# Attention slots rebuilt around three batches at a time, weights and rows transposed by DMA

## What is computed

```python
x = x + tanh(g_xattn[0]) * xattn(layernorm(x), ctx_512, Wq, Wkv_expand, Wout)
x = x + tanh(g_ffn[0]) * ffn(layernorm(x), w_gate_up, w_down)

# xattn: 16 heads of 32, causal, softmax over the keys
qp, (k, v) = q @ Wq.T, split(latent_kv @ Wkv_expand.T)
attn = softmax(where(causal, (qh @ kh.T) / sqrt(32), lowest)); out = (attn @ vh) @ Wout.T
# ffn, I = 1408; every operand is rounded to 255 steps of its row's maximum
gate, up = split(quant(x) @ quant(w_gate_up).T)
return quant(silu(gate) * up) @ quant(w_down).T
```

## Time and profile before

| what | us |
|---|---|
| time, median of 3 runs (lowest, highest) | 884.68 (880.06, 885.18) |
| the profiled execution's own time | 884.49 |
| its span, from the first to the last instruction | 882.4 |
| busy: PE 782.7 (89%), DVE 638.7 (72%), POOL 518.5 (59%), ACT 418.2 (47%) | of 882.4 |
| mean granted TensorE clock | 0.955 of full |

### The profile page before, as it was taken

One profiled execution on the slowest core, in us unless ns is written; L12 is line 12 of the kernel. 1 busy time (PEld: TensorE's weight loads), 2 busy tenths in 40 slices (PEclk: granted clock), 3 DMA queues, 4 the chain that ended last, 5 costly groups with the idle time before them and its releaser, 6 DMA issues. The chain is left out here.

```text
span 882.4 us, 19003 instructions
## 1 busy us (share of the span) xinstructions
PE 782.7 (89%) x6146; PEld 564.8 (64%) x6168; DVE 638.7 (72%) x1997; ACT 418.2 (47%) x664; POOL 518.5 (59%) x671
## 2 busy tenths in 40 slices
PE   2579899998999989989999999897699999999994
PEld 2468787886877877868878778675444444444441
DVE  3575776876866867768678576476389999999992
ACT  5336456466375464563664645414234444444441
POOL 3525466474564663754745637324167888888885
PEclk9788899999999999999999999977899999999998
DMA  5784765775857757768668575406115655565666
GB/s 211 176 195 130 173 164 150 179 191 140 212 150 180 173 161 164 179 147 204 168 164 190 144 179 124 125 2 269 61 23 117 160 151 140 139 139 139 144 140 168
DMA packets 121889, 135.98 MB, mean 154 GB/s; under 512 B 73536, under 2 KB 84288, under 8 KB 121536
## 3 DMA queue, kind: packets, MB, share of 16 engines
q1 hardware_dynamic: 120768, 134.26, 60.0%
q10 hardware_dynamic: 1024, 0.53, 0.2%
HBM read 47.06 MB, written 25.30 MB: 82 GB/s over the span
## 5 line engine op out<-in xcount | busy, mean ns | idle before, releaser
L654 DVE CUSTOM_DVE_ANT_0 junk<-psum,mask 128x128 f32<-128x128 f32 (+1 forms) x512 | 159.4, 354 | 5.0 <-PE psum L843 3.2
L1172 PE MATMUL psum<-w1q,xqb 128*128 128x512 bf16 (+1 forms) x757 | 157.7, 363 | 3.3 <-PEq L255 1.9
L1072 POOL TENSOR_TENSOR up<-gate,up 128x512 f32<-128x512 f32 (+1 forms) x96 | 112.4, 1185 | 46.1 <-ACT gate L1098 38.3
L390 POOL TENSOR_SCALAR_AFFINE_SELECT prob<-prob 128x512 f32<-128x512 f32 x128 | 80.2, 638 | 94.5 <-ACT prob L588 87.0
L1172 PEld LDWEIGHTS psum<-w1q,xqb 128*128 128x128 bf16 x768 | 75.4, 98 | 83.9 <-issue 4.0
L1103 ACT ACTIVATE up<-up,round_bias,hinv 128x1408 f32<-128x1408 f32 x32 | 50.0, 1561 | 128.7 <-DVE hinv L1144 128.7
L588 ACT ACTIVATE prob<-psum 128x768 f32<-128x768 f32 x128 | 101.5, 827 | 18.4 <-PE psum L912 18.0
L910 PE MATMUL psum<-qs,ks 98*128 98x256 f32 x256 | 78.8, 369 | 23.8 <-DMA qs<-nmT 18.6
L1186 PE MATMUL psum<-w2q,hqT 128*128 128x512 bf16 x341 | 81.8, 389 | 7.4 <-DMA hqT<-hq 6.8
L910 PEld LDWEIGHTS psum<-qs,ks 98*128 98x128 f32 x256 | 50.8, 199 | 44.6 <-DMA qs<-nmT 25.9
L843 PE MATMUL psum<-ks,qs 96*128 96x256 f32 x256 | 76.1, 344 | 0.0
(11 more groups left out here) (126 smaller groups left out, 1904.2 us busy)
## 6 DMA issues: line engine op xcount, KB each, us to landing
ks<-k_hi SPq DMA_DIRECT2D x128, 128.0 KB, 2.7
qs<-q_hi SPq DMA_DIRECT2D x128, 128.0 KB, 2.4
xln<-x_dram SPq DMA_DIRECT2D x16, 512.0 KB, 5.0
ks<-k_lo SPq DMA_DIRECT2D x64, 128.0 KB, 2.5
qs<-q_lo SPq DMA_DIRECT2D x64, 128.0 KB, 2.9
x<-x_dram SPq DMA_DIRECT2D x16, 512.0 KB, 3.9
x_scratch<-x SPq DMA_DIRECT2D x16, 512.0 KB, 5.1
x1b<-x_scratch SPq DMA_DIRECT2D x32, 256.0 KB, 3.5
```

Of the source, the lines that this page charges most:

```text
L390: pool.affine_select(out=blk, in_=blk, compare_op=ALU.is_ge, fill=0.0, base=0, pattern=[[0, 4], [1, P]], channel_multiplier=-1).then_inc(s ...
L654: dve.tensor_tensor_reduce(junk[:, n % 2, 0:w], psum[:, h % 4, cols], m, 1.0, LOWEST, ALU.add, ALU.max, mx[:, par, t, h:h + 1]).then_inc(s ...
L1072: pool.tensor_tensor(up[:, t % 3, o], gate[:, t % 3, o], up[:, t % 3, o], ALU.mult).then_inc(f["prod_done"], 1)
L1172: last = pe.matmul(psum[:, n, 0:w], xqb[:, t % 4, k, :], w1q[:, k, half * I + o:half * I + o + w], start=(k == 0), stop=(k == KH - 1))
```

## The change

Slots run from b = -2 to 16, all with whole numbers. In slot b there are now batch A = b in the pairs, N = b + 1 in the scores and maxima, F = b + 2 in normalisation, transposes and all projections, T = b - 1 in the output projection. Scores use banks 0 and 1 (head h waits for the maxima of head h - 2), pairs banks 2 and 3 (each pair waits for the exponential before). Both phases stand interleaved on TensorE; the scores begin behind the fourth pair. The bf16 transposes of xq and of weight pieces on TensorE, their copies on VectorE, and the 26 scale matmuls go away: pieces are stored as they are, and `dma_start_transpose` loads w1q, w2q and each `xqb`; the scales go through DRAM and come back as broadcast rows. The weights lie where the projections' operands lay, so they are loaded in slot 14, when the last q, k and v are made. Both blocks become one, and tile 0 of the feed-forward stands between slots 15 and 16. `stand_alone` (a semaphore increment behind some waits) goes.

```diff
-            for b in range(-3, B + 2):
-                slot(b, b % 2, b // 2)
+        def run(eng, slot, tile):
+            for b in range(-2, B):
+                slot(b)
+            tile(0)
+            slot(B)
+            for t in range(1, NT + 4):
+                tile(t)
...
-        WORK = [("K", 0, 1), ("K", 1, 1), ("Q", 0, 1), ("BC", 0, -1), ("BC", 1, -1), ("Q", 1, 1), ("V", 0, 1),
-                ("XT", 0, -2), ("O", 0, -1), ("O", 1, -1), ("V", 1, 1), ("XT", 1, -2), ("T", 0, 2), ("T", 1, 2),
-                ("W", 0, 1), ("W", 1, 1)]
+        WORK = [("O", 0, -1), ("O", 1, -1), ("T", 0, 2), ("T", 1, 2), ("K", 0, 2), ("K", 1, 2), ("Q", 0, 2),
+                ("BC", 0, 0), ("Q", 1, 2), ("BC", 1, 0), ("V", 0, 2), ("V", 1, 2)]
```

```diff
+                def load_x(tile):
+                    sp.wait_ge(s["xq_stored"], DMA * (tile // ST + 1))
+                    sp.dma_start_transpose(xqb[:, tile % 4], xq_scratch[tile]).then_inc(f[f"x_loaded{tile % 4}"], DMA)
...
+                    if b == B - 2:
+                        sp.wait_ge(s["q_moved"], DMA * MOVES * B)
+                        sp.wait_ge(s["k_moved"], DMA * MOVES * B)
+                        sp.wait_ge(s["v_done"], 2 * B)
...
+                        sp.dma_start_transpose(w1q[:], w1_scratch).then_inc(f["w1_loaded"], DMA)
+                        sp.dma_start(s1[:], rows[:, 0:2 * I].broadcast_to((P, 2 * I))).then_inc(f["steps_loaded"], DMA)
+                        sp.dma_start(s2[:], rows[:, 2 * I:NW * P].broadcast_to((P, H))).then_inc(f["steps_loaded"], DMA)
+                        sp.dma_start_transpose(w2q[:], w2_scratch).then_inc(f["w2_loaded"], DMA)
+                        for tile in range(2):
+                            load_x(tile)
```

The order of a slot on GpSimd:

```diff
+                    split_context()
+                    rsqrt1()
+                    weights()
+                    if b == -2:
+                        tables()
+                    select(0)
+                    select(1)
+                    low_t(0)
+                    select(2)
+                    select(3)
+                    low_t(1)
+                    select(4)
+                    rsqrt2()
+                    select(5)
+                    low_k(0)
+                    select(6)
+                    select(7)
+                    low_k(1)
+                    low_o(0)
+                    quantise(0)
+                    low_o(1)
+                    quantise(1)
```

On ScalarE:

```diff
+                    if b > -2:
+                        weights()
+                    exps(0)
+                    norm1(0)
+                    exps(1)
+                    norm1(1)
+                    exps(2)
+                    high_t(0)
+                    exps(3)
+                    copy_u(0)
+                    exps(4)
+                    high_t(1)
+                    exps(5)
+                    norm2(0)
+                    copy_u(1)
...
+                    exps(6)
+                    high_k(0)
+                    exps(7)
+                    norm2(1)
+                    copy_u(2)
+                    high_k(1)
+                    copy_u(3)
+                    high_q(0)
+                    maxima_rows()
+                    high_o(0)
+                    high_q(1)
+                    high_o(1)
+                    copy_v(0)
+                    copy_v(1)
```

On VectorE:

```diff
+                    measure_x()
...
+                    residual(0)
+                    measure(0)
+                    residual(1)
+                    measure(1)
+                    for h in range(12):
+                        maxima(h)
+                    reciprocals()
+                    maxima(12)
+                    maxima(13)
+                    split_q(0)
+                    maxima(14)
+                    maxima(15)
+                    negate()
+                    step(0)
+                    normalise(0)
+                    split_q(1)
+                    normalise(1)
+                    step(1)
+                    weigh_rows(b + 3)
```

On TensorE, the wait of `scores(h)`, that of `score_pair(pair)`, and the order:

```diff
+                            wait_for(pe, s["max_done"], 2 * (NHEAD * N + h - 1))
...
+                        wait_for(pe, s["exp_done"], PAIRS * A + pair)
...
+                    output(0, 0)
+                    output(0, 1)
+                    score_pair(0)
+                    output(1, 0)
+                    score_pair(1)
+                    output(1, 1)
+                    score_pair(2)
+                    transposed(0)
+                    score_pair(3)
+                    weigh(0)
+                    scores(0)
+                    scores(1)
+                    score_pair(4)
+                    transposed(1)
+                    scores(2)
+                    scores(3)
+                    score_pair(5)
+                    weigh(1)
+                    scores(4)
+                    scores(5)
+                    score_pair(6)
+                    keys(0)
+                    scores(6)
+                    scores(7)
+                    score_pair(7)
+                    weigh(2)
+                    scores(8)
+                    scores(9)
+                    keys(1)
+                    scores(10)
+                    scores(11)
+                    weigh(3)
+                    queries(0)
+                    scores(12)
+                    scores(13)
+                    queries(1)
+                    scores(14)
+                    scores(15)
+                    queries(2)
+                    maxima_rows()
+                    broadcast(0)
+                    queries(3)
+                    broadcast(1)
+                    values(0)
+                    values(1)
```

More of the change, by code:

```diff
@@ new lines, in gated_block @@
+        mx = keep("mx", [P, 2, ST, NHEAD], F32)
+        nm = keep("nm", [P, ST, 2, NHEAD], F32R)
+        nmT = keep("nmT", [2 * NHEAD, S], F32R)
+        prob = keep("prob", [P, 2, 2, CAUSAL // P, 2, P], F32)
+        u = keep("u", [P, GROUPS, S], F32)
+        o_hi = keep("o_hi", [P, GROUPS, S], F32R)
+        o_lo = keep("o_lo", [P, GROUPS, S], F32R)
+        rec = keep("rec", [P, S], F32)
+        rec_hi = keep("rec_hi", [P, S], F32R)
+        rec2 = keep("rec2", [P, S], F32R)
+        x1 = keep("x1", [P, ST, H], F32)
@@ L337, in _ @@
+                run(sp, slot, tile)
+                for p in range(2):
+                    sp.wait_ge(f[f"stored{p}"], DMA * NT // 2)
             @block.gpsimd
@@ L422, in slot @@
-                    first = isinstance(b, int) and b == -2
-                    if first:
-                        split_context()
-                    if present(b + 1):
-                        for m in range(2):
-                            pool.wait_ge(s["k_copied"], 2 * (b + 1) + m + 1)
-                            wait_for(pool, s["k_moved"], DMA * MOVES * (b + 1))
-                            pool.tensor_tensor(k_lo[:, 2 * m:2 * m + 2, :], both[:, 2 * m:2 * m + 2, :],
-                                               k_hi[:, 2 * m:2 * m + 2, :].bitcast(F32), ALU.subtract).then_inc(s["k_lo"], 1)
@@ L1094, in silu, with tile @@
+                def tile(t):
                     def silu(c):
@@ L1106, in slot, with low_weights @@
                     silu(2)
-                run_tiles(act, slot)
+                run(act, slot, tile)
             @block.vector
             def _(dve):
-                dve.wait_ge(f["steps"], NSTEPS)
-                def slot(t):
+                dve.memset(round_bias[:], ROUND).then_inc(s["table"], 1)
+                def low_weights(n, hi, lo, raw):
+                    dve.wait_ge(s["high"], n + 1)
+                    dve.tensor_tensor(lo[:], raw, hi[:].bitcast(F32), ALU.subtract).then_inc(s["split"], 1)
@@ L1188, in slot @@
                         last.then_inc(f["d_done"], 1)
-                run_tiles(pe, slot)
+                run(pe, slot, tile)
 def kernel(x, ctx_512, g_xattn, g_ffn, L0_xattn_Wq, L0_xattn_Wkv_expand, L0_xattn_Wout, L0_ffn_w_gate_up,
```

1272 lines of the change are left out of this document (538 added, 734 removed).

## The result

The changed kernel takes 945.27 us (median of 4 runs, 944.4 to 946.37) where the kernel before takes 884.93 (4 runs, 880.06 to 886.74): ratio 1.0695, 95% interval 1.0657 to 1.0734. It is about 7% slower. The forecast was 897.0 with a range up to 932, so the sign was right and the size far off. The profiled execution has a span of 943.5 us.

What follows compares the result with a forecast made beforehand. Attention slots paced by TensorE's matmul starts plus handoff waits, 36.7 us each: 64.4 + 513.8 + 59.4 = 637.6 to the first feed-forward matmul, plus 246.7 + 10.6 gives span 894.9, plus 2.1 gives 897.0 us; range 858 to 932.

Steps and rivals of the forecast that it cites:

- The slot by handoffs: One attention slot followed engine by engine: 28.9 us of TensorE work plus 7.7 of stalls, the two ways meeting at 36.5.
- First stretch: Slot's start, work banks 6 and 7: TensorE waits for split_q(1) ahead of values(0); stall 2.1 us in all.
- Second: Score pairs 0 to 5, each waiting for the exponential before it, and weigh(0): stall 1.6 us.
- Third stretch: GpSimd's late rsqrt2 delays norm2(0) on ScalarE, hence exps(6) and pair 7 on TensorE: stall 2.5 us.
- rival A: GpSimd reaches rsqrt2 3.1 us earlier, the third stall goes: slot 34.4 us, 865 us in all; chance 0.24.
- Rival B: Waits merely change places, the slot stays 35.2 us as before: 876 us in all; chance 0.14.
- Fourth: Slot's end: split_q(0) holds queries(2), the end of the maxima holds their transposition: stall 1.5 us.
- I put one in ten here: TensorE's half clock behind pair 7's still stretch, assumed in one slot of ten: 0.2 us a slot.
- Rival C: TensorE's clock falls in every slot, +2.0 us each: 925 us in all; chance 0.14.
- 59.4 together: Slots 14 and 15, which lack projections, taken as 32 and 27.4 us up to tile(0).
- the paragraph on SyncE: SyncE's queue in a slot: 24 head spreads, 15 us, the last queries' hidden by 2.6 us; xq's store behind them.
- rival D: Transposed weights come late for the feed-forward: 7 us, 904 us in all; chance 0.08.

Runs made afterwards that it cites:

- e3: The changed kernel with GpSimd doing rsqrt2 ahead of low_t(1) and select(4) instead of behind them: 908.59 us.
- e7: On e5, the slot's last stretch reordered: queries(2) in the other work bank, values(0) ahead of broadcast(1), q_hi(1) and v(0) copied earlier: 900.70 us.
- e10: On e9, last stretch reordered: broadcast(0) ahead of scores(14), normalise(0) ahead of maxima(14), split_q(0) behind the negation, both low_o ahead of quantise: 872.80 us.
- e11: On e10, in slot -2 GpSimd rounds weights behind low_t(1) and writes the tables behind low_k(1): 867.39 us.
- e9: On e4, the scales are turned by TensorE and stored as 26 rows of 512 bytes instead of 3,328 elements of 4 bytes: 878.58 us.
- e1: The changed kernel with VectorE gating w2's scales in slot 4, not at the end of slot 13; store unmoved: 924.08 us.
- e2: The changed kernel with the scale store moved to the end of SyncE's slot 13, its wait kept: 931.78 us.
- e12: On e9, three extra unread stores of constants: 512 elements in slot 4, 3,328 in slot 7, 128 rows of 104 bytes in slot 10: 883.78 us.
- e4: The changed kernel with both edits of e1 and e3 (w2's scales gated in slot 4, rsqrt2 early): 886.40 us.
- e5: On e4, the scale store cut up: two columns in each w1 piece's slot, w2's four in slot 5: 898.23 us.
- e6: On e5, in slot -2 GpSimd rounds weights behind low_t(1) and writes the tables behind low_k(1): 894.07 us.

## Why the prediction was right or wrong

The slot by handoffs: right. Without a fall of the clock it takes 36.79 us, forecast 36.5. First stretch: the gap ahead of values(0) is 1.77 us, forecast 1.76 (0.24 to 2.0). Second: pair 3 starts 12.3 us behind the last queries, forecast 12.5. Third stretch: GpSimd's rsqrt2 holds norm2(0) by 2.88 us and pair 7 by 1.95, forecast 3 and 2.5, and e3 shows it as a cause: with rsqrt2 ahead of low_t(1) the slot is 34.55. That is rival A's number, 34.4; its condition, GpSimd 3.1 us earlier, wasn't met. Rival B fell with the same rows. Fourth: 1.02 us at queries(2), in the changed kernel as in e3, forecast 1.5 for the whole stretch. e7 and e10 show that these waits aren't worth their length: with them moved or shortened, the slot was no shorter.

The clock: mechanism right, size wrong. "I put one in ten here" was a mis-sized term. The clock falls in every second slot from slot 4 on, 1.5 us each, and twice in slots 1 and 2, which take 3.8 and 2.6 us more than 36.79: together 14 us, where 14 x 0.2 = 2.8 were counted. That is 11 of the 12.7 us of the slots; 0.29 us a slot are 4 more, and slot 0, counted as a full one though it has no batch T and no output projection, gives 2.6 back net. Rival C had every slot. The window of before, 0.54 behind 2.79 of 5 us, was read as an exception; read slot by slot, the kernel before has such falls in slots 1, 5 and 12 of 0 to 13. e3 ties the falls to the gap ahead of pair 7 by taking it away: every second slot became three in fourteen. What is enough of a gap is not shown: e10 and e11, with 0.32, 0.60, 0.30 and 0.79 us in the last stretch, have no fall in slots 1 to 13, but e7, with 1.15, 0.89 and 0.78, has eight.

Start: the q spreads were in at 49.4 us, forecast 48.5. The other 4 us of the 4.7 lie in slot -1, at half clock from 48 to 61 us, which the step "VectorE's 16 heads and the two queries banks then bring the end of slot -1 to 64.4" had at full pace.

Slots 14 and 15: "59.4 together" was right to 2.4 us for what it counted. In e9 the stretch from the copy of slot 13 to the first feed-forward matmul is 63.4 us (619.08 less 555.70), in e10 61.1, forecast 61.0. In the changed kernel it is 91.4. The step that failed is the paragraph on SyncE: "Queued behind them is the store of xq, which nothing awaits for 25 us." It listed what is queued in an ordinary slot, and the count of slots 14 and 15 struck out the 26 scale broadcasts without asking what replaces them. That one store in slot 13 was put at nothing: neither its wait for VectorE's last instruction of the slot, ahead of 24 spreads (27.1 us of slot 14 by e1), nor its own 3,328 elements (7.8 us by e9, if the wait isn't there to hide it). No rival had it either, so the range ended 13 us under the result. The direction doesn't hang on it: without these 30.4 us the kernel would take some 915 us, an estimate from the table, slower than before and inside the range.

Weights by DMA: right, nothing late. The transposes landed 14.7 and 13.9 us after their issue, and both were in 26.2 us after the first was issued (647.41 + 13.9 - 635.13), where 43.2 was the serial price by the earlier trace rows. Their issues took 11.14 and 10.00 us (16.6 forecast for both), and each landed 3.6 to 3.9 us behind the end of its own. So issue sets the pace, and rival D falls, in e9 too, where no hole gives the loads time:

```profile
w1q<-w_scratch SPq DMA_TRANSPOSE x1, 14.7
w2q<-w_scratch SPq DMA_TRANSPOSE x1, 13.9
```

The Trainium skill (VectorE: DVE Perf Modes, "The three transpose paths") gives 1309 ns for a block by DMA; here 88 blocks came in 14.7 us, 0.17 us each, so the measurement decides against taking that price serially.

Feed-forward: right. 258.1 us, forecast 257.3, with tiles that start 7.13 us apart on TensorE, transposed loads of x beside them:

```profile
863.56 4.92 PE L1062 MATMUL psum<-w1q,xqb 128*128 128x512 bf16 x23
870.69 4.92 PE L1062 MATMUL psum<-w1q,xqb 128*128 128x512 bf16 x24
```

The forecast that the wait for the maxima's DMA goes is right too: nobody waits for it in the trace.

## What to carry to other kernels

An in-order queue has to be walked for every slot that differs from the ordinary one: the instruction that cost most here is executed once, and the wait ahead of it held 24 transfers. Make the awaited thing early (one condition, 27 us in slot 14). To put the wait behind what the next stage needs helps less: in e2 it then held the load of x that stood behind it. A hand chain of handoffs was exact to 1% for the slot, so the first thing to repair was the gap that it named; but gaps taken away in an exchange over two banks left the slot no shorter, twice (e7, e10). Turn small columns into rows before they are stored.

## What the runs showed of the hardware

- A store of 3,328 elements of 4 bytes, 13 KB, took 17.4 us to land with the DMA engines at a share of 1.08 and 15 GB/s, and issues behind it on the same queue took 8.14 us for 0.56 (e12). The same bytes as 128 rows of 104 bytes cost nothing measurable.
- Beside stores of 4-byte columns engines can stand still without a visible wait: TensorE 3.04 us in e4, with ScalarE and VectorE; all four for most of 275 to 280 us in e5; ScalarE 4.69 us behind 512 elements in e12. The kernels without such a store have no such wait over 1 us, nor have the changed kernel and e3, where it is issued just ahead of the hole. What is waited for is open.
- Behind the same gap of 1.93 to 1.95 us on TensorE the granted clock fell to 0.58 in one slot and stayed at full in the next, slot after slot (changed kernel, slots 3 to 13). Behind 1.6 to 1.8 us it fell in three slots of fourteen (e3), behind gaps like 0.94 and 0.78 us close together in eight of thirteen (e7). With none over 0.8 (e11's slot from 366 to 402 us) it stayed at full.
- A phase that TensorE does alone, with short gaps, can run at half clock from end to end: 13 us in slot -1 in the changed kernel, 14 us in e6. The kernel before has 12 us of it, with longer gaps.
